# Conditional residual matmul on one core: the bias table split once, first transposes and loads rearranged, early stores issued later

## What is computed

```python
# x (128, 64, 256), cat (128,) int32 in 0..63, W (64, 256, 256), b (64, 256), all float32
selected_W = W[cat_ids]
selected_b = b[cat_ids]
out = jnp.einsum('bsd,bdh->bsh', x, selected_W) + selected_b[:, None, :]
return x + out
```

## Time and profile before

| | us |
|---|---|
| median of 3 runs | 100.14 (100.07 to 100.21) |
| the profiled execution | 100.16 |
| its span, first to last instruction | 98.40 |
| PE busy | 88.4 |
| DVE busy / ACT busy / POOL busy | 57.4 / 56.4 / 33.6 |
| moved by DMA | 31.19 MB, mean 317 GB/s |

### The profile page before, as it was taken

How to read it: one execution, slowest core, us unless ns; L and a number is a source line. 1 busy time by engine, 2 the same in 40 slices (tenths; PEclk the granted TensorE clock), 3 DMA queues, 4 the chain that set the end, 5 groups by cost and what they waited for, 6 DMA issues and landing times.

```text
span 98.4 us, 3042 instructions
## 1 busy us (share of the span) xinstructions
PE 88.4 (90%) x788; PEld 58.6 (60%) x788; DVE 57.4 (58%) x139; ACT 56.4 (57%) x98; POOL 33.6 (34%) x63
## 2 busy tenths in 40 slices
PE   0229499999999999999999999999999999999980
PEld 0126257666666667676757575857676767676740
DVE  2736430688787693747466665666555646463840
ACT  4102426965834756766676764867585858585500
POOL 5100000000000029999986566785323480000000
PEclk9999999999999999999999999999999999999999
DMA  1999999999999998899999999999998799996363
GB/s 18 340 308 343 353 350 349 348 351 350 348 353 351 349 348 242 258 333 315 395 361 393 358 406 358 400 388 388 376 386 290 208 330 320 347 336 205 110 210 110
DMA packets 19891, 31.19 MB, mean 317 GB/s; under 512 B 1505, under 2 KB 15906, under 8 KB 19874
## 3 DMA queue, kind: packets, MB, share of 16 engines
q0 software_dynamic: 4640, 16.26, 46.8%
q1 hardware_dynamic: 13330, 12.91, 40.9%
q10 hardware_dynamic: 1904, 1.84, 5.9%
HBM read 25.23 MB, written 8.39 MB: 342 GB/s over the span
## 4 chain that ended last, share of the span: by engine, by line
PE 85%; DMA 7%; DVE 2%; issue 1%; SPq 1%; ACT 1%; POOLq 0%; DVEq 0%
PE mm_ps L584 56%; PE xt_ps L492 17%; PE mm_ps L570 8%; DMA w_all<-in_L_cond_W 6%; PE mm_ps L498 2%; PE xt_ps L584 2%; DMA cats_i<-in_itok_B 1%; SPq L169 1%; ACT w_slot L327 1%; DVE rows L461 0%; DVE same_ahead L409 0%; PE mm_ps L503 0%; DVE has_place L421 0%; PE mm_ps L510 0%; DVE cats L401 0%
## 5 line engine op out<-in xcount | busy, mean ns | idle before, releaser
L584 PE MATMUL mm_ps<-w_slot,xT 128*64 128x256 f32 x496 | 58.0, 386 | 0.6 <-ACT w_slot L327 0.6
L327 ACT COPY w_slot<-w_all 128x512 f32 x64 | 39.0, 619 | 26.1 <-PE mm_ps L584 9.7
L584 PEld LDWEIGHTS mm_ps<-w_slot,xT 128*64 128x64 f32 x496 | 34.7, 139 | 18.0 <-issue 1.3
L461 DVE TENSOR_TENSOR rows<-mm_ps,rows 128x512 f32<-128x512 f32 (+1 forms) x32 | 21.6, 675 | 28.2 <-PE mm_ps L584 27.8
L183 POOL DMA_DIRECT2D w_all<-in_L_cond_W x32 | 16.4, 515 | 40.2 <-DMA w_all<-in_L_cond_W 33.6
L327 DVE COPY w_slot<-w_all 128x512 f32 x64 | 26.7, 454 | 3.6 <-POOLq L199 3.0
L339 ACT COPY xT<-xt_ps 128x512 f32<-128x512 f32 x32 | 17.3, 584 | 8.9 <-PE xt_ps L492 8.9
L492 PE MATMUL xt_ps<-ident,rows 128*128 128x128 f32 x128 | 19.2, 298 | 0.0
L492 PEld LDWEIGHTS xt_ps<-ident,rows 128*128 128x128 f32 x128 | 15.1, 151 | 6.8 <-issue 6.8
L570 PE MATMUL mm_ps<-bias_parts,is_sample 96*64 96x256 bf16 x124 | 10.3, 288 | 0.7 <-ACT xT L339 0.7
L214 POOL DMA_DIRECT2D out<-rows x11 | 8.8, 800 | 1.1 <-issue 0.6
(11 more groups left out here) (46 smaller groups left out, 12.8 us busy)
## 6 DMA issues: line engine op xcount, KB each, us to landing
w_all<-in_L_cond_W POOLq DMA_DIRECT2D x32, 256.0 KB
w_all<-in_L_cond_W SPq DMA_DIRECT2D x28, 256.0 KB, 6.1
out<-rows POOLq DMA_DIRECT2D x11, 512.0 KB, 8.1
rows<-in_x POOLq DMA_DIRECT2D x9, 512.0 KB, 7.2
rows<-in_x SPq DMA_DIRECT2D x6, 512.0 KB, 6.7
out<-rows SPq DMA_DIRECT2D x8, 256.0 KB, 4.0
w_all<-in_L_cond_W ACTq DMA_DIRECT2D x4, 256.0 KB, 5.8
rows<-in_x ACTq DMA_DIRECT2D x1, 512.0 KB, 3.9
```

What stands on the lines that cost most here:

```text
L327: copy(w_slot[:, PAIR * p + half, :, :].rearrange("p k h -> p (k h)"), w_all[:, bass.ds(c, 1), :, :].rearrange("p c k h -> p (c k h)")).th ...
L461: V.tensor_tensor(to, sums, to, ALU.add).then_inc(sums_added, 1)
L584: last = T.matmul(to[HALF * half:HALF * (half + 1), :], xT[:, slot, k, j, :], w_slot[:, j, k, :], start=False, stop=(k == K - 1), skip_gro ...
```

## The change

1. The bias table is loaded twice (64 KB each, into the lower and the upper 64 partitions of `bias_nat`; the first by SP ahead of group 0 of x, the second by ACT ahead of group 1). DVE splits the whole table once into three bf16 parts. PE gathers a tile by two bf16 products (`bias_two` with `in_two`, then `bias_third` with `in_third`) in place of one float32 product; three selections are made in place of one, on buffers that POOL sets to zero. DVE then only copies a gathered tile out (`put_tile`).
2. Tile 0 is gathered behind the transposes of group 0, and tiles 1 to 3 behind pair 0. DVE's copies of the weights of pairs 1 to 3 of group 0 have a `put_tile` behind each, and the later ones wait for the gathered tile.
3. The transposes of group 1 stand ahead of the bias of group 0.
4. ACT issues loads 0, 6 and 7, the latter two behind its copies of group 0's halves; SP issues 1 to 5.
5. POOL issues load 32 when 27 loads are reported, not 29.
6. POOL stores groups 0 to 5 after loads 40, 43, 46, 48, 51, 55 in place of 37, 40, 43, 46, 48, 51. The order of x is as it was.

```diff
-REPORTED_FIRST = 29
+REPORTED_FIRST = 27
+ACT_LOADS = (0, 6, 7)
-STORE_AFTER_LOAD = {0: 37, 1: 40, 2: 43, 3: 46, 4: 48, 5: 51, 6: 59}
+STORE_AFTER_LOAD = {0: 40, 1: 43, 2: 46, 3: 48, 4: 51, 5: 55, 6: 59}
@@ SP @@
+            sp.dma_start(bias_nat[0:C, :], bias).then_inc(bias_loaded, 16)
             load_rows(sp, 0)
-            sp.dma_start(bias_nat[:, :], bias).then_inc(bias_loaded, 16)
             load_rows(sp, 2)
...
-                if n < FIRST_LOADS and n % PAIR == 0:
+                if n in ACT_LOADS:
                     continue
@@ POOL @@
+            pool.memset(in_two[:, :, :, :], 0.0).then_inc(masks_set, 1)
+            pool.memset(in_third[:, :, :, :], 0.0).then_inc(masks_set, 1)
@@ ACT @@
+            act.dma_start(bias_nat[C:PAIR * C, :], bias).then_inc(bias_loaded, 16)
             load_rows(act, 1)
...
-            for n in range(PAIR, FIRST_LOADS, PAIR):
...
-                load_weights(act, n, part(word, n % WORD))
             for k in range(K):
                 x_half(0, k)
+            for n in ACT_LOADS[1:]:
+                load_weights(act, n, part(word, n % WORD))
@@ DVE @@
-            V.tensor_scalar(in_category[:, :, :, :], cat_row[0:C, :].rearrange("c (t n) -> c t n", n=TILE)
-                            .unsqueeze(2).broadcast_to([C, TILES, SPLITS, TILE]),
-                            iota_part[0:C, 0:1], None, ALU.is_equal).then_inc(plan_step, 1)
+            dve.wait_ge(bias_loaded, 32)
...
+            split(V.tensor_copy(bias_two[:, :], bias_nat[:, :]))
+            split(V.tensor_tensor(bias_rest[:, :], bias_nat[:, :], bias_two[:, :], ALU.subtract))
+            V.tensor_copy(bias_two[lower, :], bias_rest[lower, :]).then_inc(plan_step, 1)
+            split(V.tensor_copy(bias_second[:, :], bias_rest[upper, :]))
+            V.tensor_tensor(bias_third[:, :], bias_rest[upper, :], bias_second[:, :], ALU.subtract).then_inc(plan_step, 1)
+            dve.wait_ge(masks_set, 2)
+            V.tensor_scalar(in_two[upper, :, 0, :], tiled[upper], iota_part[upper, 0:1], None, ALU.is_equal
+                            ).then_inc(plan_step, 1)
...
+            def put_tile(t):
+                V.tensor_copy(bias_parts[:, t, :], bias_ps[t]).then_inc(bias_ready, 1)
...
             for p in range(PAIRS_IN_GROUP):
                 copy_weights(dve, V.tensor_copy, slots[p], 0, p, 0, even_weights_ready)
+                if p >= 1:
+                    dve.wait_ge(tiles_made, 1 if p == 1 else TILES - 1)
+                    put_tile(p)
@@ PE @@
-                return T.matmul(bias_ps[t], in_category[:, t, :, :].rearrange("c a n -> c (a n)"), bias_nat[:, :],
-                                start=True, stop=True)
+                T.matmul(bias_ps[t], in_two[:, t, :, :].rearrange("c a n -> c (a n)"), bias_two[:, :],
+                         start=True, stop=False, skip_group_check=True)
+                return T.matmul(bias_ps[t], in_third[:, t, :, :].rearrange("c a n -> c (a n)"), bias_third[:, :],
+                                start=False, stop=True, skip_group_check=True)
...
-                if 1 <= g < GROUPS - 1:
+                if g < GROUPS - 1:
                     transpose_next()
...
                     if g == 0 and pair == 0:
-                        transpose_next()
+                        for n in range(1, TILES):
+                            bias_of_tile(n).then_inc(tiles_made, 1)
```

More of the change, by code:

```diff
@@ L31 @@
 FAR = 1000.0
-PLAN_STEPS = {"samples": 6, "cats": 7, "first": 10, "list": 13, "slots": 16, "bias": 17}
+PLAN_STEPS = {"samples": 6, "cats": 7, "first": 10, "list": 13, "slots": 16, "bias": 21}
 X_AFTER_LOAD = {3: 13, 4: 19, 5: 25, 6: 31, 7: 33, 8: 37, 9: 40, 10: 43, 11: 46, 12: 48, 13: 51, 14: 55, 15: 60}
-STORE_AFTER_LOAD = {0: 37, 1: 40, 2: 43, 3: 46, 4: 48, 5: 51, 6: 59}
+STORE_AFTER_LOAD = {0: 40, 1: 43, 2: 46, 3: 48, 4: 51, 5: 55, 6: 59}
 POOL_GROUPS = 11
@@ L62, in build_cond_residual @@
     assert FAR == 1000.0 and BITS <= 7
-    assert B == P and S == HALF and D == H == 2 * P and C == 2 ** BITS and WORD * BITS <= 24
+    assert B == P == PAIR * C and S == HALF and TILES == 2 * PAIR and D == H == 2 * P and C == 2 ** BITS and WORD * BITS <= 24
     assert WEIGHT_SLOTS == GROUP and PAIRS_IN_GROUP == WORD and C % LOADS_IN_FLIGHT == 0
@@ L134, in build_cond_residual @@
         cat_col_ps = mm_ps[3][:, 0, B:B + 1]
-        bias_ps = [mm_ps[r % BANKS][0:ROWS, 0, :] for r in (2, 4, 6, 8)]
+        bias_ps = [mm_ps[2 + t // PAIR][0:ROWS, t % PAIR, :] for t in range(TILES)]
         cats_loaded = sem("cats_loaded")
@@ L146, in build_cond_residual @@
         plan_read = sem("plan_read")
+        masks_set = sem("masks_set")
         tiles_made = sem("tiles_made")
@@ L429, in _, with split @@
             assert steps[0] == PLAN_STEPS["slots"]
-            V.tensor_scalar(in_category[:, :, :, :], cat_row[0:C, :].rearrange("c (t n) -> c t n", n=TILE)
-                            .unsqueeze(2).broadcast_to([C, TILES, SPLITS, TILE]),
-                            iota_part[0:C, 0:1], None, ALU.is_equal).then_inc(plan_step, 1)
-            steps[0] += 1
+            dve.wait_ge(bias_loaded, 32)
+            splits = [0]
+            def split(instruction):
+                splits[0] += 1
+                instruction.then_inc(bias_step, 1)
+                dve.wait_ge(bias_step, splits[0])
+            upper, lower = slice(0, C), slice(C, PAIR * C)
+            split(V.tensor_copy(bias_two[:, :], bias_nat[:, :]))
[4 more added lines that the diff above has]
+            dve.wait_ge(masks_set, 2)
+            tiled = cat_row.rearrange("c (t n) -> c t n", n=TILE)
+            V.tensor_scalar(in_two[upper, :, 0, :], tiled[upper], iota_part[upper, 0:1], None, ALU.is_equal
+                            ).then_inc(plan_step, 1)
+            V.tensor_scalar(in_two[lower, :, 1, :], tiled[lower], float(C), iota_part[lower, 0:1], ALU.add, ALU.is_equal
+                            ).then_inc(plan_step, 1)
+            V.tensor_scalar(in_third[:, :, 2, :], tiled[upper], iota_part[upper, 0:1], None, ALU.is_equal
+                            ).then_inc(plan_step, 1)
+            steps[0] += 5
             assert steps[0] == PLAN_STEPS["bias"]
@@ L438, in _ @@
             slots = slots_of(mybir.EngineType.DVE, 0, 0)
-            splits = [0]
-            def split(instruction):
-                splits[0] += 1
-                instruction.then_inc(bias_step, 1)
-                dve.wait_ge(bias_step, splits[0])
[L447 to L455, removed]
+            def put_tile(t):
+                V.tensor_copy(bias_parts[:, t, :], bias_ps[t]).then_inc(bias_ready, 1)
             dve.wait_ge(plan_products, 5)
-            split_bias(0, bias_ps[0])
+            put_tile(0)
             def add_rows(to, sums):
@@ L519, in _ @@
             last.then_inc(plan_products, 1)
-            pe.wait_ge(plan_step, PLAN_STEPS["bias"])
-            pe.wait_ge(bias_loaded, 16)
-            bias_of_tile(0).then_inc(plan_products, 1)
             pe.wait_ge(x_loaded[0], 16)
@@ L527, in _ @@
                 transpose_half(0, k)
+            pe.wait_ge(plan_step, PLAN_STEPS["bias"])
+            bias_of_tile(0).then_inc(plan_products, 1)
             def group(g):
```

28 lines of the change are left out of this document (11 added, 17 removed).

## The result

| | before | after |
|---|---|---|
| median, us | 100.17 (100.07 to 101.49) | 105.09 (103.67 to 106.89, 4 runs) |
| the profiled execution | 100.16 | 103.67 |
| its span | 98.40 | 101.8 |
| DVE's last addition ends | 96.14 | 97.46 |
| last store has landed | 97.9 | 101.3 |

The changed kernel is slower. The prediction, 98.5 with a range up to 103.3, was wrong, in sign and in range. Profiled executions don't all lie at their kernel's median (this one is its kernel's shortest run), so the trace is read for places and durations, and verdicts rest on the ratios.

The account below looks back on a forecast made before the run. PE was taken to bound the kernel, running without a gap from 12.37 us, with loads close behind. Savings at the start were capped by load 31: 100.16 - 1.65 = 98.5, own range 98.0 to 99.4, whole range 97.9 to 103.3.

Parts of the forecast that it names:

- the loads cap the gain: Loads of weights stand less than two microseconds behind PE at 20 to 40 us; lead beyond 1.65 is waited away.
- load 31: Pair 19's odd matrix: its copy lets pair 19 start at 38.75 at the earliest, against 40.4, a gain of 1.65.
- the load of pair 15: The load whose ACT copy stood at 32.41 before the change: caps the gain at 2.2 in the same way.
- the start: Pair 0 at 12.2 (11.3 to 12.7); transposes of group 2 at 16.5 to 17.6 in place of 19.48.
- The six products: The bf16 products for tiles 1 to 3, behind pair 0: 0.14 each, 0.84 in all (0.42 to 1.80).
- The lead that the start gives: At group 4: 1.9 to 3.0 from the start plus 1.80 from the float32 tiles, 3.7 to 4.8.
- the order of the first transposes: Group 1's transposes (1.90) move from behind pair 0 into PE's idle time ahead of it.
- PE's level: PE's clock, 1.2 or 2.4 GHz by durations at the start: pair 0 takes 0.87 to 1.98.
- rival A: At 36 to 40 us POOL's stream crowds out SP's last transfers, group 6 of x late: 99.7 to 104.0; chance 0.46.
- the stores: POOL's waits for stores: 5.7 per step, last x at 84.5, wanted 85.1; slower above 5.82 (rival B, chance 0.05).
- A cover of 0.6 us: At the last group of x: landed at 84.5, PE wants it at 85.1.

Follow-up runs that it names:

- e1: The changed kernel with the old places of the stores (groups 0 to 5 after loads 37, 40, 43, 46, 48, 51): 99.12 us, ratio 0.990 to the kernel before.
- e9: e5 with a filler ahead of pair 0, group 0 transposed a second time into PSUM that is overwritten unread: 99.3 us, ratio 0.991 to the kernel before.
- e10: The kernel before with POOL's first load after 27 reports in place of 29, nothing else: 100.5 us, ratio 1.001 to the kernel before.
- e5: e1 with the transposes of group 1 back behind pair 0 and the bias tiles: 101.75 us, ratio 1.016 to the kernel before.
- e11: The changed kernel without its stores of groups 9 and 10 (1 MB of the result not written): 103.38 us, ratio 1.029 to the kernel before.
- e12: The changed kernel again, unaltered, run for comparison with e11: 105.15 us, ratio 1.049 to the kernel before.
- e8: e1 with the bias table loaded once, three bf16 products of 32 columns gathering a tile, one selection: 100.06 us, ratio 0.997 to the kernel before.
- e6: The changed kernel, but POOL issues the store ahead of the group of x that stands after the same load: 99.40 us, ratio 0.994 to the kernel before.

## Why the prediction was wrong, point by point

**Right: that the loads cap the gain. Wrong: which load.** Pair 19 starts at 39.06 (forecast 38.75), a gain of 1.3 and not 1.65. The forecast let load 31 stop PE there, and the load of pair 15 cap at 2.2. In the trace PE is stopped at pair 15 (1.15 us, a cap of 1.4) and loses 0.02 at pairs 16 to 19. Load 31's copy ends at 38.88, so it would have held PE at 39.02 had pair 15 not done so. That both caps come out within 0.1 of each other, and near the forecast, is luck. e1 and e9 show that a surplus of lead is waited away ahead of these loads, and e10 that the cap is not felt without one. By the same sum e1, the change without its stores, should end at 98.5; it ended at 99.1 (99.02 profiled). Of the 0.5, 0.4 is pair 19's (39.19 in e1, forecast 38.75) and 0.1 lies between there and the last addition.

**Right in direction, off in size: the start.** Pair 0 came at 12.78 (12.2 forecast, 12.7 the far end). The six products took 1.43 (0.84 forecast, 1.80 the far end): I had let two of them stream at once, and they did not. The lead that the start gives, 1.5 at group 2 and three tiles of 0.60, is 3.3, under the 3.7 to 4.8 of the text. None of it reached the sum. One point was missed: SP's own stream runs 0.8 later from the start (group 3 of x is issued at 15.1, before at 14.3), so SP comes later to its first reports; ACT's copy for pair 15 starts at 33.21 and not at 32.41, which is how its cap comes to 1.4.

**Right for a reason not given: the order of the first transposes.** I treated PE's level as a range of 0.87 to 1.98 for pair 0. e5 and e9 show that filling the pauses ahead of pair 0 is worth 2.4 us in all, more than anything else in the start, and e5's one trace puts it down to PE's level.

**Wrong: rival A, 0.46.** Group 6 of x took 7.1 us (7.3 in the earlier trace rows), with POOL's stream 1.1 us ahead of where it was (35.26 against 36.31 in the earlier trace rows), and PE transposed it at 40.0. The page DMA: Bandwidth & Descriptors of the Trainium skill (section "Queues, rings and completion order") has the engines take turns between queues by packets; by the prediction's reading of that rule group 6 would have landed at 45.3. The measurement decides: it landed at 39.6. The rule may hold, but the lean of bytes in the earlier trace rows was no measure of what one transfer in flight pays.

**The step that failed: the stores.** The text had the mechanism, the condition and the point from which it decides, 5.82 us per step, and gave it 0.05. Its terms:

| | forecast | measured |
|---|---|---|
| store of group 0 has landed | 51.0 | 52.3 |
| x issue and going on | 1.1 | 1.06 |
| a store to its landing, mean of the next five | 4.6 | 5.02 |
| step | 5.7 | 6.08 |
| last x issued | 79.5 | 83.0 |
| its landing takes | 5 | 4.9 |
| last x has landed | 84.5 | 87.9 |

Of the 3.5 us at the issue of the last x, 1.3 is the first store (issued 0.3 later than forecast, and 7.9 to land, forecast 6.9 from the earlier trace rows), 0.3 is the time to go on behind it, and 1.9 is five times 0.38, the step's excess (0.42 more for the landing, 0.04 less for the rest). The value of 4.6 was the earlier trace rows, one store issued when the loads were nearly over, the lower of two ends of which the upper was 6.9. A cover of 0.6 us over five steps is 0.12 for a step, on a term known to within 2.3. The sum took the end nearer to the forecast, and so did the chance. With the measured step and first store, the prediction's own sum is 98.5 + (87.9 - 85.1) = 101.3.

**What was not priced at all.** The text counted what a thin queue does for a store, not what it does to the rest. While POOL waits it issues nothing; 2 MB are left over, and the stores behind the last x, which SP and POOL issue from 84.8 on, find each other in the queue: SP's stores of 256 KB take 7.2 us to land in the median, 4.1 before the change. That is 2.0 us behind the last addition (e11) beyond 101.3, together 103.3 of the profiled 103.67. In e12's trace, 105.39, the steps are longer still (6.34), the last addition ends 0.6 later, and the last landing comes 5.1 and not 3.8 behind it.

## What to carry to other kernels

Ask of an issue order how many transfers may be in flight when a queue's engine stops to wait. Here a store that stands behind the wait for the store before it turns a stream with two in flight into a chain of one issue and one landing per step, and exchanging two neighbouring lines is 5.6 us of 100. When a chain of that kind has five steps, its margin is the margin of one step, so take the duration from the dearer row; and count what piles up behind it, since bytes not moved in the middle come back at the end. At the start, an idle PE is worth filling: with the pauses filled, by useful work or not, the products behind them ran at twice the pace.

## What the runs showed that I had not expected

- In e5, PE ran without a pause from 13.35 us on, and its eight transposes at 17.51 still took 1.97; in e9 and e1 the level rose at about 13 to 14 us, after unbroken work from 7.8. The kernel before, with pauses of 0.68 and 0.64 in their place, had it up for most of pairs 1 to 3, which start at 16.2 (3.23 for 24 records). The granted clock reads full speed (1.00) in all of these stretches. The durations of equal work tell the level, and that line doesn't.
- Two products that write the same 96 rows of PSUM followed each other at 0.24 (13.79 to 15.22 for six). In e8, three of 32 columns each, into three blocks of 32 rows, ran together (PE in order of time, one tile and the first product of the next):

```profile
15.40 0.28 PE L498 MATMUL mm_ps<-bias_first,in_category 64*32 64x256 bf16 x1
15.40 0.28 PE L498 MATMUL mm_ps<-bias_second,in_category 64*32 64x256 bf16 x1
15.41 0.28 PE L498 MATMUL mm_ps<-bias_third,in_category 64*32 64x256 bf16 x1
15.52 0.27 PE L498 MATMUL mm_ps<-bias_first,in_category 64*32 64x256 bf16 x1
```

  A tile takes 0.12 so, against 0.48. The page TensorE: Matmul & The Clock Gate of the Trainium skill (section "Part 3: Packing small matmuls — row/col tiling") says that products in different column groups of the array run at the same time; the trace agrees.
- A store of 512 KB took 4.6 to 5.8 us to land when it was the only one and 6.0 in the median with a second one in flight (e6), so two at a time move more than one; the first one of the changed kernel, in a full queue, took 7.9.
